# A graph layer on one core: one more short turn of two j-tiles, another split of the row sums, and one evacuation behind its split

## The reference, cut to what matters

```python
def _gcn_layer(x, adj, W, b):
    d_inv_sqrt = (jnp.sum(adj, axis=1) + 1e-09) ** (-0.5)
    msg = d_inv_sqrt[:, None] * adj * d_inv_sqrt[None, :] @ x
    return jax.nn.relu(msg @ W + b)
H_f = _gcn_layer(feature_x, adj, W_f, b_f)
H_s = _gcn_layer(spatial_x, adj, W_s, b_s)
attn = jax.nn.sigmoid(jnp.concatenate([H_f, H_s], axis=1) @ W_att + b_att)
out = _layernorm(x + attn * H_f + (1.0 - attn) * H_s)
```

## Time and profile before

| | us |
|---|---|
| median of 3 runs (392.58 to 392.72) | 392.65 |
| the profiled execution, device time | 392.9 |
| its span, from the first to the last instruction | 391.1 |
| PE busy / DVE / ACT / GpSimd | 376.7 / 303.1 / 285.3 / 157.4 |
| granted TensorE clock, mean | 0.995 |
| read from HBM | 128.32 MB |

### The profile page before, as it was taken

How to read it: one execution, slowest core, us unless ns; L and a number is a source line. 1 busy time by engine, 2 the same in 40 slices (tenths; PEclk the granted TensorE clock), 3 DMA queues, 4 the chain that set the end, 5 groups by cost and what they waited for, 6 DMA issues and landing times. The chain is left out here.

```text
span 391.1 us, 5491 instructions
## 1 busy us (share of the span) xinstructions
PE 376.7 (96%) x1778; PEld 312.8 (80%) x1778; DVE 303.1 (78%) x441; ACT 285.3 (73%) x379; POOL 157.4 (40%) x204
## 2 busy tenths in 40 slices
PE   7789999999999999999999999999999999999992
PEld 7567878788887788888888888888788888888992
DVE  2789996999576884879579593928976796889795
ACT  3677888788877887888878886778742666687656
POOL 2334512670065512771159200110100417877795
PEclk9999999999999999999999999999999999999998
DMA  8999999999999999999999999999675534455002
GB/s 272 421 418 423 421 419 415 424 418 418 422 416 422 421 421 418 421 419 421 421 420 422 421 416 421 415 408 386 250 271 211 213 108 152 172 159 165 4 25 81
DMA packets 24556, 130.77 MB, mean 334 GB/s; under 512 B 2640, under 2 KB 7632, under 8 KB 10448
## 3 DMA queue, kind: packets, MB, share of 16 engines
q1 hardware_dynamic: 24528, 130.43, 83.1%
HBM read 128.32 MB, written 2.10 MB: 333 GB/s over the span
## 5 line engine op out<-in xcount | busy, mean ns | idle before, releaser
L533 DVE TENSOR_TENSOR Al<-raw,Ah 128x2048 fp32r<-128x2048 f32 (+2 forms) x99 | 161.3, 1642 | 36.7 <-ACT Ah L720 36.6
L408 PE MATMUL sums<-Ah,Yh 128*128 128x512 f32 (+1 forms) x488 | 188.5, 386 | 1.2 <-DVE Al L533 1.0
L410 PE MATMUL sums<-Al,Yh 128*128 128x512 f32 (+1 forms) x488 | 186.6, 382 | 0.0
L409 PE MATMUL sums<-Ah,Yl 128*128 128x512 f32 (+1 forms) x488 | 186.6, 382 | 0.0
L720 ACT ACTIVATE Ah<-raw 128x2048 fp32r<-128x2048 f32 (+2 forms) x99 | 126.8, 1306 | 51.2 <-DMA raw<-in_At 31.9
L730 ACT ACTIVATE nat<-nat 128x2048 f32<-128x2048 f32 (+1 forms) x54 | 100.1, 1854 | 19.7 <-DMA nat<-in_adj 18.7
L408 PEld LDWEIGHTS sums<-Ah,Yh 128*128 128x128 f32 x488 | 91.7, 188 | 22.8 <-DVE Al L533 3.7
L410 PEld LDWEIGHTS sums<-Al,Yh 128*128 128x128 f32 x488 | 91.7, 188 | 18.0
L409 PEld LDWEIGHTS sums<-Ah,Yl 128*128 128x128 f32 x488 | 91.8, 188 | 17.1
L553 DVE TENSOR_TENSOR acc<-sums,acc 128x512 f32<-128x512 f32 (+1 forms) x122 | 77.1, 672 | 32.1 <-PE sums L410 29.5
L870 POOL TENSOR_TENSOR S<-S,raw 128x512 f32<-128x512 f32 x40 | 64.5, 1614 | 30.3 <-DMA raw<-in_At 27.2
(11 more groups left out here) (56 smaller groups left out, 192.4 us busy)
## 6 DMA issues: line engine op xcount, KB each, us to landing
raw<-in_At SPq DMA_DIRECT2D x63, 1024.0 KB, 9.3
nat<-in_adj SPq DMA_DIRECT2D x47, 1024.0 KB, 11.6
nat<-in_adj SPq DMA_DIRECT2D x8, 768.0 KB, 9.6
xs<-in_xs SPq DMA_DIRECT2D x5, 512.0 KB, 10.5
out<-xs SPq DMA_DIRECT2D x15, 128.0 KB, 1.8
xs<-in_xs SPq DMA_DIRECT2D x5, 256.0 KB, 11.6
nat<-in_adj SPq DMA_DIRECT2D x2, 512.0 KB, 6.8
raw<-in_At SPq DMA_DIRECT2D x2, 512.0 KB, 8.7
```

Source lines behind the costliest of these rows:

```text
L408: pe.matmul(to, Yh[:, t % YRING, hs], high, start=first, stop=False)
L409: pe.matmul(to, Yl[:, t % YRING, hs], high, start=False, stop=False)
L410: mm = pe.matmul(to, Yh[:, t % YRING, hs], low, start=False, stop=last)
L533: dve.tensor_tensor(Al[:, k % SPLITS, a * IB:b * IB], raw[:, k % RAWS, a * IB:b * IB], Ah[:, k % SPLITS, a * IB:b * IB], ALU.subtract).the ...
```

## The change

One more turn of two j-tiles stands among the early ones: the j-tiles of the turns are now [0], [0, 1], [1, 2], [2, 3], [3, 4], [4, 5] and [5, 6, 7], in items 0, 1-2, 3-4, 5-6, 7-8, 9-10 and 11-13. The front has 64 runs instead of 60. Every turn from item 14 on falls to the other set: groups 4 to 7 (with GpSimd's groups 6 and 7) have items 14-17, 22-25 and so on, where they had 18-21, 26-29. The last column (items 46, 47) is that of groups 4 to 7. The j-tiles of the items are as before but for items 9 and 10: t4 and t5 instead of t5 and t4, t5. `parts` follows: parts 10 and 11 stand at item 10 (at item 9 before), 12 at item 11 (10), 13 at 12 (11), 14 and 15 at 13 (12 and 13); from part 16 on nothing moves.

GpSimd sums j-tiles 2 to 21: it has no blocks in items 1 and 2, two blocks each in items 9, 10, 14 to 17, 22 to 25 and so on, up to 38 to 41, where before they stood in items 1, 2, 5, 6, 10 to 13, 18 to 21 and so on up to 34 to 37 (5 and 6 stay). The count of 40 is the same. Parts 48 to 55 have the columns 0 to 255 and 2816 to 4095, in two DMAs each (128 and 640 KB).

Items 20 and 21 are split in two pieces like items 14 to 19. In a column item among 14 to 21 the third evacuation moves behind the second piece.

```diff
-HALVED = 20
+HALVED = 22
-    for n, tiles in enumerate([[0], [0, 1], [1, 2], [2, 3], [3, 4, 5]]):
+    for n, tiles in enumerate([[0], [0, 1], [1, 2], [2, 3], [3, 4], [4, 5], [5, 6, 7]]):
         spread(add_runs(sets[n % 2], tiles, range(4)), tiles)
-    for n in range(3, FRONT // 2):
+    for n in range(4, FRONT // 2):
         old, fresh = [2 * n - 2, 2 * n - 1], [2 * n, 2 * n + 1]
-        new = add_runs(sets[n % 2], old + fresh, range(4))
+        new = add_runs(sets[(n + 1) % 2], old + fresh, range(4))
...
-    column(add_runs(sets[0], tiles, [0, 1, 2, 0]), tiles)
+    column(add_runs(sets[1], tiles, [0, 1, 2, 0]), tiles)
...
-    SUMMED = range(5 * GT)
-    PLAIN_FROM = len(SUMMED) * P
+    SUMMED = range(2, 22)
+    PLAIN = [(0, SUMMED[0] * P), ((SUMMED[-1] + 1) * P, N)]
+    PLAIN_COLS = sum(b - a for a, b in PLAIN)
...
-    parts[4], parts[6], parts[8], parts[9] = [4, 5], [6, 7], [8, 9], [10, 11]
-    for n in range(12, 30):
+    parts[4], parts[6], parts[8], parts[10] = [4, 5], [6, 7], [8, 9], [10, 11]
+    parts[11], parts[12], parts[13] = [12], [13], [14, 15]
+    for n in range(16, 30):
         parts[n - 2].append(n)
...
         def nat_here(eng, n):
-            eng.wait_ge(nat_in[n % NATS], 16 * (n // NATS + 1))
+            pieces_in = sum(len(PLAIN) if m >= 2 * FULL else 1 for m in range(n % NATS, n + 1, NATS))
+            eng.wait_ge(nat_in[n % NATS], 16 * pieces_in)
...
-                    sp.dma_start(nat[:, n % NATS, 0:N - PLAIN_FROM],
-                                 adj_r[r, :, PLAIN_FROM:N]).then_inc(nat_in[n % NATS], 16)
+                    c = 0
+                    for a, b in PLAIN:
+                        sp.dma_start(nat[:, n % NATS, c:c + b - a], adj_r[r, :, a:b]).then_inc(nat_in[n % NATS], 16)
+                        c += b - a
...
-                        if STEPWISE <= k < HALVED:
+                        if STEPWISE <= k < HALVED and items[k][0][0] != items[k][1][0]:
                             evacuate_new(ending[:3])
...
-                h, width = (n % 2, N // 2) if r < FULL else (0, N - PLAIN_FROM)
+                h, width = (n % 2, N // 2) if r < FULL else (0, PLAIN_COLS)
```

## The result

| | before | after |
|---|---|---|
| median, us | 392.8 (392.58 to 393.28, 22 runs) | 393.31 (393.12 to 394.36, 22 runs) |
| ratio | | 1.0014 [1.0008, 1.0021] |
| profiled execution, us (span) | 392.9 (391.1) | 393.12 (391.3) |

The change costs 0.5 us. That is within the 0.2% of "no change" and within the range, but it has the other sign than the forecast of -0.15 us, and the interval of the ratio leaves 1 out. So at least one of the steps behind -0.15 us is wrong.

What follows compares the result with a forecast made beforehand. PE, busy 96% of the span, was taken as the bound, losing 5.1 us to DVE's late output. -0.15 + 1.6 - 1.9 + 0.3 = -0.15 us gave 392.5 us against a median of 392.65, range 390.8 to 394.0.

Steps and rivals of the forecast that it cites:

- Blocks gone from items 1 and 2: Item 3 starts nearly 2 us earlier, but DVE's load leaves only -0.15 us at item 8 (0 to -0.2).
- The added turn: Items 8 and 9: DVE's pieces, held by GpSimd's blocks, cost PE 0.6 and 1.0 us, together +1.6 (+0.5 to +2.5).
- Turns by the other set: Items 10 to 21: without GpSimd's blocks until item 14 and with `HALVED` = 22, PE's waits go, -1.9 us.
- Item 15: Four evacuations and GpSimd's blocks together in items 14 to 17 cost +0.3 us at item 15 (0 to 1.1).
- Behind that the trace shows nothing of this kind that the change touches: Behind the start of item 21, no PE waits that the change touches; 5.1 us are all there is to win.
- GpSimd's last blocks in items 38 to 41: Moved from item 37 to 41, wanted behind item 42, with landings far ahead of PE: cost nothing.
- The split DMAs: Eight more 128 KB DMAs for the row sums cost nothing, being in time even if late one after another (14.4 us).
- item 50 did not wait: Sign: if item 50, the first that uses t28, waited for Yh, the forecast on the split DMAs was wrong.
- The faster one: Rival: GpSimd's blocks slip between splits in items 8 and 9, costing 0.5 us; 391.05 us in all, chance 0.36.
- The slower one: Rival: DVE is pushed past PE in items 8 to 11 and 15, over 1.9 us; up to 394.3 us, chance 0.15.
- the moved waits: Rival: waits before items 20 and 21 move to 22 and 23, 1.0 us not won; 393.4 us, chance 0.08.

Runs made afterwards that it cites:

- e1: The changed kernel run again with no edit, for a second profile: 393.44 us, ratio 1.0017.
- e4: The changed kernel with GpSimd's two blocks of item 5 cut from 512 to 16 columns: 393.64 us, ratio 1.0022.
- e6: The kernel before with items 20 and 21 halved and the third evacuation moved behind the split in column items: 392.58 us, ratio 0.9995.
- e7: The kernel before with items 20, 21 halved, the third evacuation moved, and the two parts in front of item 33 instead of 27: 392.03 us, ratio 0.9982.
- e5: The changed kernel with GpSimd's eight blocks of items 38 to 41 cut to 16 columns: 392.87 us, ratio 1.0007.
- e11: The changed kernel with `HALVED` at 20 instead of 22: 393.15 us, ratio 1.0009.
- e3: The changed kernel with two parts in front of item 39 instead of 27: 392.98 us, ratio 1.0001.
- e9: The changed kernel with the two parts in front of item 33 instead of 27: 393.19 us, ratio 1.0007.
- e8: The changed kernel with parts 48 to 55 loaded in one DMA each: 393.36 us, ratio 1.0016.
- e12: The changed kernel with the third evacuation back where it was, ahead of the second piece in column items: 393.37 us, ratio 1.0015.
- e2: The kernel before with all the change's edits except the added turn, keeping old turns and parts: 394.04 us, ratio 1.0028.
- e10: The changed kernel with two parts before item 33 instead of 27 and GpSimd's blocks of items 38 to 41 at 16 columns: 392.7 us, ratio 0.9999.

## Why the prediction was wrong, step by step

**Blocks gone from items 1 and 2: right in kind.** Item 3 starts at 30.17 (29.78 in e1; 29.4 expected), and the third piece of item 4 gives it back. DVE's split, and PE waiting for it:

```profile
36.83 2.19 DVE L538 TENSOR_TENSOR Al<-raw,Ah 128x1024 fp32r<-128x1024 f32 x1 [0.18 <-ACT Ah L725]
```

```profile
39.08 0.50 PE L413 MATMUL sums<-Ah,Yh 128*128 128x512 f32 x1 [0.59 <-DVE Al L538]
```

e4 shows the block of item 5 to be the cause of that wait. The size was wrong: not -0.15 us at item 8, but +0.32 and +0.56. After's PE comes to item 4 1.30 us earlier than before's, but DVE's rows from 38.95 to 46.08 are those of before (38.94 to 46.07), and PE falls back to DVE's pace. What is left over, +0.32 us, begins with the degree of a row tile on GpSimd. First before, then after, GpSimd and DVE:

```profile
43.54 0.30 POOL L828 TENSOR_SCALAR dg<-rs 128x1 f32<-128x1 f32 x1 [3.37 <-ACT nat L730]
...
46.07 1.11 DVE L533 TENSOR_TENSOR Al<-raw,Ah 128x512 fp32r<-128x512 f32 x1
```

```profile
43.70 1.35 POOL L833 TENSOR_SCALAR dg<-rs 128x1 f32<-128x1 f32 x1 [3.52 <-ACT nat L735]
...
46.08 1.42 DVE L538 TENSOR_TENSOR Al<-raw,Ah 128x512 fp32r<-128x512 f32 x1
```

Before, the degree (0.30 us) had begun 0.19 us ahead of DVE's split at 43.73. In after it came 0.16 us later, met that split (43.75) and took 1.35 us; the blocks behind it began at 45.65 instead of 45.34, and DVE's next piece ended 0.32 us later. This need not be the change's doing: e6 and e7, which have the old plan, show a degree of 1.36 us too, and their item 8 starts at 59.35 and 59.55. The profile of before was the lucky one.

**The added turn: right, the size too high.** Item 9 landed at 57.2, as worked out, and item 8 went as written: first piece done at 59.07, Yl at 60.51, last at 62.24.

```profile
57.72 1.35 DVE L538 TENSOR_TENSOR Al<-raw,Ah 128x512 fp32r<-128x512 f32 x1
59.00 1.51 DVE L547 SCALAR_TENSOR_TENSOR Yl<-xs,D,Yh 128x256 fp32r<-128x256 f32 x1
60.43 1.81 DVE L538 TENSOR_TENSOR Al<-raw,Ah 128x512 fp32r<-128x512 f32 x2
```

Items 8 and 9 lost 0.42 + 0.26 = 0.68 us instead of 1.6 (e1: 0.67). Item 9 depends on the phase, that is on when GpSimd's blocks begin against DVE's pieces. (e5 cuts only blocks from item 38 on.) In after GpSimd's blocks of item 10 began at 65.63, before the last piece at 66.96, which took 1.21 us and PE lost 0.26. In e5 they began at 66.40, the piece at 66.82 took 1.94 us, and PE lost 1.00. e4 is like e5 there (blocks from 66.38, the piece 1.95 us) and lost 1.03 us in item 9; it lost 0.86 in item 8 as well, which it began 0.6 us earlier. The ten profiles with the added turn have 0.65 to 0.78 us for the two items in eight cases, 1.37 in e5 and 1.89 in e4. So the 1.6 us, worked out with every piece held, lay within what can come, but was over twice what mostly came.

**Turns by the other set: the size right, one cause wrong.** Items 10 to 21 lose nothing instead of 1.99 us; -1.9 was forecast. I gave half of it to `HALVED`; e11 shows that in this plan the moved blocks do it. e6 shows that in the old plan the halves are enough, with the moved evacuation. Either would have done.

**Item 15: +0.3 forecast, 0 measured.** No wait from item 10 to 25 at all.

Up to here the steps leave a lead of 1.0 us at item 22 (0.76 in e1), more than the 0.15 us of the sum. That the measured change still came within 0.7 us of the forecast one is luck: 0.6 to 0.8 us too little in these steps stand against 1.2 to 1.7 us left out behind them.

**The step that failed** is the sentence "Behind that the trace shows nothing of this kind that the change touches", with "nothing" for GpSimd's last blocks in items 38 to 41. A timeline of PE shows where PE waits; it doesn't show how much sooner PE could come before it would wait. I made that check for one landing, that of item 22 (2.2 us to spare), and left out item 27, the only one with two parts in front, whose row stood in the trace of before with 0.67 us to spare. It took 0.6 us in after and 0.9 in e1; e3 and e9 take the wait away. For items 38 to 41 I looked at when the sums are wanted, and not at DVE, whose whole splits are 2.28 us long and pay 0.8 us each. It took 0.4 and 0.55 us; e5 takes it away, and so does the other moment at which the blocks fall in e3 and e9. In e3 and e9 a third limit then takes the lead, the landing of item 47; e5 has 392.87 us, 0.44 less than after. With the 0.2 us in the tail: -0.99 + 0.59 + 0.44 + 0.2 = +0.2 us, the profiled execution of after, and -0.76 + 0.92 + 0.55 + 0.2 = +0.9, that of e1. The median, +0.5 us, lies between. The split DMAs did no harm that counts in after; item 50 did not wait. The prediction's estimate from the Trainium skill (DMA: Bandwidth & Descriptors, Measured, 0.95 us for a DMA of 64 KB) was some 8 us on the DMA engines for the eight small pieces. Nothing of that size is seen: six of them stand before item 47, and it landed 0.6 to 1.3 us later than in e8.

**The rivals.** None happened as written. The faster one was near for items 8 and 9 (0.5 us against 0.68 and 0.67), and its time did not come. The slower one, DVE held past PE in items 8 to 11 and 15 by over 1.9 us, did not come in after or e1; items 8 and 9 of e4 lost 1.89 us. Of the moved waits, the sense was right and the place wrong: they moved to items 26, 27, 38 and 39, not to 22 and 23, and the reason is the landing and the blocks.

**What stays open.** The times of the kernels with the new plan mostly spread over 1 us and more (0.63 us in e12, 1.24 in after, 1.94 in e11), those of before and e6 over less (0.70 and 0.26; e7 1.08 without its one far execution). The phase of blocks in items 8 and 9 and the clock behind `collect`, seen in one profile, are candidates; which it is in the single runs no profile tells. Before has one profile only, and its starts up to item 8 are the early ones of the old plan. Whether e7's parts would be better at another item than 33 was not tried.

## What to carry to other kernels

A lead of the engine that bounds the kernel is worth only what the next late landing lets through. So for each later item write down the landing and the work behind it against the time at which the engine will now ask, and begin with the items that have something extra in front (two parts, a collect, a block of another engine). If a moved load is what is in the way, it is moved more cheaply than the work: e7 gained 0.55 us against e6 by six loads standing one item later. It is worth that only if the next landing lets it through: the same move in the changed kernel (e9) took the wait away and left the time within the spread, 393.19 against 393.31 us. And of two edits that take away the same wait, one is idle; only a run with each alone shows which.

## What the runs showed of the hardware

The granted clock of PE fell to 0.5, the 1.2 GHz level, in item 0 in seven profiles (after, e3, e4, e6, e7, e9, e11; not in before, e1, e2, e5, e8, e10, e12), and once behind the 16 small matmuls of `collect` (e2). Ahead of item 0 PE had waited 2.18 us in after, but 2.46 in before, where the clock did not fall. It cost 1.6 to 1.7 us on PE where I read it (after, e6, e2). In item 0 none of it was left at item 4 (after against e1), behind `collect` all of it reached item 48.

A whole split by DVE took 2.28 us alone, 2.79 beside the last two blocks (e2) and up to 3.38 beside a pair or more (after, at 234.46). The Trainium skill's rule that DVE with two SBUF inputs and GpSimd exclude each other for whole instructions (SBUF — State Buffer, SBUF: two separate sides) fits: no split was longer by more than 1.10 us, and a block takes 1.37 (2.73 / 2). What I had not expected is that GpSimd's smallest instructions pay as well. The degree of a row tile, one column, alone and beside the whole split of DVE at 234.46 (after):

```profile
215.03 0.30 POOL L833 TENSOR_SCALAR dg<-rs 128x1 f32<-128x1 f32 x1 [7.98 <-ACT nat L735]
...
235.78 2.22 POOL L833 TENSOR_SCALAR dg<-rs 128x1 f32<-128x1 f32 x1
```

The longest was 2.47 us (e10, at 247.17), 2.17 more than alone and still less than a whole split. It makes D late, and it moves the blocks behind it: in e5 a degree of 1.15 us at 64.64 is part of why the blocks of item 10 began 0.8 us later than in after and met DVE's last piece.
